# A spline feed-forward stage: pairs of knots side by side in the two 64-row halves, and TensorE takes part of the sum

## The reference, cut to what matters

```python
s = layernorm(x) @ Win + bin_                    # (2048, 64)
for h in range(16):                              # INNER = 16 knots
    g += relu(s * W1[:, h] + b1[:, h]) * W2[:, h]    # elementwise on 2048 x 64
out = (g + b2) @ Wout + bout                     # (2048, 128)
x = x + out
```

## Time and profile before

| what | value |
|---|---|
| timed runs | 2342.31, 2346.17, 2368.61 us (median 2346.17) |
| profiled execution, its own time | 2356.42 us |
| its span in the trace | 2354.6 us |
| TensorE matmuls busy over the span | 1947.0 us, 83% |
| VectorE busy | 1680.3 us, 71% |
| ScalarE busy | 1372.5 us, 58% |
| GpSimd busy | 497.5 us, 21% |
| the two spline stages | 43.44 us and 43.35 us |

### The profile page before, as it was taken

The page is one execution under the profiler, slowest core; times in us unless marked ns, Lnnn a source line. Parts: engine busy times, 40 slices in busy tenths (PEclk is TensorE's granted clock), DMA queues, the critical chain, the costliest instruction groups (busy, mean ns, idle before and its releaser), DMA issues. The chain is left out here.

```text
span 2354.6 us, 39284 instructions
## 1 busy us (share of the span) xinstructions
PE 1947.0 (83%) x13014; PEld 1053.1 (45%) x13014; DVE 1680.3 (71%) x4272; ACT 1372.5 (58%) x2027; POOL 497.5 (21%) x963
## 2 busy tenths in 40 slices
PE   4899899984899984697899899976647999999849
PEld 3433343332567763464333333356424333333348
DVE  6788788737566767567798798642697887988443
ACT  4247767766278875335367677842444467667722
POOL 4101121110266650120100111123101010210233
PEclk9579999985899996797699999978856899999959
DMA  7242130003201000005142020005114402200024
GB/s 226 78 72 27 13 39 1 2 2 125 87 26 40 38 25 1 1 1 164 16 73 38 3 38 2 2 10 198 45 36 144 69 10 34 36 4 1 2 93 176
DMA packets 48058, 117.49 MB, mean 50 GB/s; under 512 B 12400, under 2 KB 21874, under 8 KB 43592
## 3 DMA queue, kind: packets, MB, share of 16 engines
q1 hardware_dynamic: 40260, 100.02, 18.0%
q0 software_dynamic: 5088, 11.24, 1.5%
q10 hardware_dynamic: 2540, 4.09, 0.5%
HBM read 65.96 MB, written 36.20 MB: 43 GB/s over the span
## 5 line engine op out<-in xcount | busy, mean ns | idle before, releaser
L1128 ACT ACTIVATE probs<-score 128x1024 f32<-128x1024 f32 x960 | 823.6, 898 | 431.2 <-PE score L1227 425.8
L1298 DVE TENSOR_REDUCE max_part<-stat 128x1 f32<-128x512 f32 x1152 | 725.0, 684 | 95.0 <-PE stat L1179 87.0
L1241 PE MATMUL pv<-probs,v_ones 128*9 128x512 f32 (+3 forms) x3840 | 460.8, 553 | 0.2 <-ACT out_turned L1121 0.2
L1295 DVE CUSTOM_DVE_ANT_0 masked_scores<-stat,mask_row 128x128 f32<-128x128 f32 (+3 forms) x768 | 347.2, 488 | 144.9 <-PE stat L1179 141.4
L1179 PE MATMUL stat<-first_group_k,first_group_q 64*128 64x512 f32 (+2 forms) x960 | 364.3, 494 | 36.3 <-DVE max_part L1298 12.6
L1179 PE MATMUL stat<-group_k,group_q 64*128 64x512 f32 (+2 forms) x960 | 337.4, 407 | 16.1 <-DVE max_part L1298 7.6
L1179 PEld LDWEIGHTS stat<-first_group_k,first_group_q 64*128 64x128 f32 x960 | 176.3, 215 | 284.2 <-DVE max_part L1298 176.5
L1179 PEld LDWEIGHTS stat<-group_k,group_q 64*128 64x128 f32 x960 | 157.6, 185 | 278.6 <-DVE max_part L1298 162.9
L1227 PE MATMUL score<-first_group_q,first_group_k 64*128 64x512 f32 x960 | 249.6, 420 | 32.0 <-ACT probs L1128 19.5
L1227 PE MATMUL score<-group_q,group_k 64*128 64x512 f32 x960 | 232.2, 423 | 40.1 <-ACT probs L1128 30.8
L1086 POOL TENSOR_SCALAR_AFFINE_SELECT probs<-probs 128x256 f32<-128x256 f32 x384 | 150.2, 408 | 238.3 <-ACT probs L1128 237.1
(11 more groups left out here) (424 smaller groups left out, 2567.8 us busy)
## 6 DMA issues: line engine op xcount, KB each, us to landing
tile_wv<-expert_wv SPq DMA_DIRECT2D x38, 512.0 KB
q_parts<-early_parts_t SPq DMA_DIRECT2D x14, 512.0 KB, 3.7
group_k<-k_parts SPq DMA_DIRECT2D x24, 256.0 KB, 11.8
group_q<-q_parts SPq DMA_DIRECT2D x24, 256.0 KB, 18.4
sorted_rows<-in_c_unused_rows SPq DMA_DIRECT2D x1, 4754.5 KB, 25.2
k_parts<-early_parts_t SPq DMA_DIRECT2D x8, 512.0 KB, 4.6
head_q<-q_parts SPq DMA_DIRECT2D x32, 128.0 KB
head_k<-k_parts SPq DMA_DIRECT2D x32, 128.0 KB
```

What stands on the lines that cost most here:

```text
L1128: nc.scalar.activation(probs[:, n % PSLOTS, :, 0:width], sc[m % 2][:, :, 0:width], ACT.Exp, scale=scale).then_inc(slot_read.sem, 1)
L1241: last = nc.tensor.matmul(acc[32 * h:32 * h + D + 1, f:BANK], v9[:, kt, g * HG + h, :], probs[:, (2 * t + h // 2) % PSLOTS, h % 2, 0:BANK ...
L1295: nc.vector.tensor_tensor_reduce(masked[:, at % 2, 0:width], ring[n % RBANKS][:, 0:width], w["mask_row"][:, BANK - width:BANK], 1.0, NEG, ...
L1298: nc.vector.reduce_max(into, ring[n % RBANKS][:], AX.X).then_inc(stat_used.sem, 1)
```

## The change

The two 64-row halves no longer hold different tokens but different knots of the same tokens. `Win` is loaded twice, side by side (128 columns), so that one matmul for each quarter writes s into both halves of a bank of `spline_in_ps`. Rows 0 to 63 of W1, b1 and W2 hold knots 0 to 7, rows 64 to 127 knots 8 to 15; one 128x512 instruction works on a pair of knots of one quarter. There are 8 pairs times four quarters, again 32 units. They are divided:

- pair 7 (`OWN`) is bent by VectorE itself, straight from PSUM, as max(W1 s, low) with low = -(W1 bin + b1); the constant that this leaves out goes into b2. TensorE sums it.
- pairs 5 and 6 (`BY_PE`) are bent by ScalarE and summed by TensorE: the knot tile is multiplied by `folded` = W2 times Wout, three 128x128 tables which VectorE makes in the stage (with `bias`, `low` and `b2`).
- pairs 0 to 4 (`BY_SUM`) are bent by ScalarE and added by VectorE into one running sum, which waits for its direct predecessor. There is no even and odd sum and no join.

ScalarE reads `spline_in_ps` (PSUM) with a bias that holds bin, so `enter` is gone; its knots of a quarter wait for VectorE's own knot of that quarter (`own_knots`). `spline_in_ps` grows from two banks to four. In each quarter TensorE has four products of 512 tokens (own pair, pair 5, pair 6, sum with `Wout`) that accumulate in one bank over all 128 rows. The four quarters end one after another, and the statistics of a quarter follow in the next quarter's adds. The normalisation order is 0, 1, 2, 3 in place of 0, 2, 1, 3, and TensorE transposes the third quarter ahead of the first feed.

In `experts_stage` three semaphores become one; the five GpSimd instructions and their order stay.

```diff
 rest_loads
-        (w["Win"][:], d["L0_ffn_Win"]),
+        (w["Win"][:, 0:M0], d["L0_ffn_Win"]),
+        (w["Win"][:, M0:], d["L0_ffn_Win"]),
+        (w["b2"][0:M0, :], d["L0_ffn_b2"].rearrange("(m o) -> m o", o=1)),
+        (w["b2"][M0:, :], d["c_pad"][0, 0:M0].rearrange("(m o) -> m o", o=1)),
...
 spline_ffn_stage
+    BY_SUM, BY_PE, OWN = (0, 1, 2, 3, 4), (5, 6), (7,)
+    BENDS = [(q, m) for q in range(NQ) for m in (0, 5, 1, 2, 6, 3, 4)]
...
             @block.tensor
+                def feed(q):
+                    norm.wait(pe, q)
+                    nc.tensor.matmul(sp_in[:, q, :], w["Win"][:], xn_t[:, q * BANK:(q + 1) * BANK], start=True, stop=True).then_inc(fed.sem, 1)
+                def take(q, lhs, weight, first, last):
+                    for i in range(QC):
+                        ins = nc.tensor.matmul(out[:, q, i * P:(i + 1) * P], lhs[:, i * P:(i + 1) * P], weight, start=first and i == 0, stop=last and i == QC - 1)
+                    return ins
+                norm.turn(pe, 0)
+                norm.turn(pe, 1)
+                norm.turn(pe, 2)
                 feed(0)
+                norm.turn(pe, 3)
+                for q in range(1, NQ):
+                    feed(q)
+                pe.wait_ge(tables.sem, tables.at(ALL_TABLES))
+                for q in range(NQ):
+                    for n in range(NO):
+                        pe.wait_ge(own_knots.sem, own_knots.at(NO * q + n + 1))
+                        take(q, own[:, q % 2, n, :], folded[:, n, :], n == 0, False).then_inc(used.sem, 1)
+                    for n, m in enumerate(BY_PE):
+                        pe.wait_ge(knots.sem, knots.at(BEND_AT[q, m] + 1))
+                        take(q, slot(q, m), folded[:, NO + n, :], False, False).then_inc(used.sem, 1)
+                    pe.wait_ge(summed.sem, summed.at(NS * (q + 1)))
+                    take(q, g[:, q % 2, :], w["Wout"][:], False, True).then_inc(out_ready.sem, 1)
...
             @block.scalar
+                def bend(n):
+                    q, m = BENDS[n]
+                    act.wait_ge(own_knots.sem, own_knots.at(NO * (q + 1)))
+                    if n >= SLOTS:
...
+                    nc.scalar.activation(slot(q, m), sp_in[:, q, :], ACT.Relu, bias=bias[:, m:m + 1], scale=w["W1"][:, m:m + 1]).then_inc(knots.sem, 1)
                 def begin(n):
+                    if n == 2:
+                        act.wait_ge(tables.sem, tables.at(BIAS))
+                        for m in range(2):
+                            bend(m)
...
             @block.vector
+                def bend(q):
+                    dve.wait_ge(fed.sem, fed.at(q + 1))
...
+                        nc.vector.tensor_scalar(own[:, q % 2, n, :], sp_in[:, q, :], w["W1"][:, m:m + 1], low[:, m:m + 1], ALU.mult, ALU.max).then_inc(own_knots.sem, 1)
+                def add(q, n):
...
+                        dve.wait_ge(summed.sem, summed.at(NS * q + n))
+                        ins = nc.vector.scalar_tensor_tensor(into, slot(q, m), w["W2"][:, m:m + 1], into, ALU.mult, ALU.add)
...
                 norm.dve(dve)
+                nc.vector.scalar_tensor_tensor(bias[:], w["W1"][:], w["bin"][:, 0:1], w["b1"][:], ALU.mult, ALU.add).then_inc(tables.sem, 1)
+                nc.vector.tensor_scalar(low[:], bias[:], -1.0, None, ALU.mult).then_inc(tables.sem, 1)
...
+                bend(0)
+                for n, m in enumerate(OWN + BY_PE):
+                    ins = nc.vector.tensor_scalar(folded[:, n, :], w["Wout"][:], w["W2"][:, m:m + 1], None, ALU.mult)
+                ins.then_inc(tables.sem, 1)
+                for q in range(NQ):
+                    for n in range(NS):
+                        add(q, n)
+                        if n == 0 and q + 1 < NQ:
+                            bend(q + 1)
+                        if n == NS - 3 and q > 0:
+                            complete(q - 1)
+                        if n == NS - 2 and q > 0:
+                            read(q - 1)
+                    if q > 0:
+                        stats.gather(dve, q - 1)
+                complete(NQ - 1)
+                read(NQ - 1)
+                stats.gather(dve, NQ - 1)
```

More of the change, by code:

```diff
@@ L1354, in _ @@
             def _(pe):
[L1355 to L1363, removed]
@@ L1365, in project @@
-                def project(c):
-                    pe.wait_ge(whole.sem, whole.at(c + 1))
-                    for half in range(2):
-                        at = slice(half * M0, half * M0 + M0)
-                        for i in range(QC):
-                            ins = nc.tensor.matmul(out[:, 2 * half + c, i * P:(i + 1) * P], g[at, c, 0, (INNER // 2) % 2, i * P:(i + 1) * P], w["Wout"][at, :],
-                                                   start=True, stop=True)
-                        ins.then_inc(out_ready.sem, 1)
@@ L1442, in complete, with read @@
                     part = x[:, QC * q:QC * q + QC, :]
                     nc.vector.tensor_tensor(part, out[:, q, :].rearrange("p (i c) -> p i c", c=C), part, ALU.add).then_inc(out_used.sem, 1)
-                    stats.follow(dve, n, out_used)
+                def read(q):
+                    dve.wait_ge(out_used.sem, out_used.at(q + 1))
+                    stats.take(q)
                 norm.dve(dve)
-                for h in range(INNER):
-                    add(0, h)
-                for h in range(2):
-                    add(1, h)
@@ L1451, in _ @@
-                join(0)
-                for h in range(2, INNER):
-                    add(1, h)
-                    if h == 9:
-                        dve.wait_ge(biased.sem, biased.at(1))
-                        complete(0)
-                    if h == 11:
-                        complete(1)
-                join(1)
-                complete(2)
-                complete(3)
-        fed.done(2)
-        s_ready.done(2)
-        whole.done(2)
-        knots.done(2 * INNER)
-        summed.done(2 * INNER)
+                nc.vector.scalar_tensor_tensor(bias[:], w["W1"][:], w["bin"][:, 0:1], w["b1"][:], ALU.mult, ALU.add).then_inc(tables.sem, 1)
@@ new lines, in _ @@
+                dve.wait_ge(tables.sem, tables.at(BIAS))
+                nc.vector.tensor_scalar(low[:], bias[:], -1.0, None, ALU.mult).then_inc(tables.sem, 1)
+                for n, m in enumerate(OWN):
+                    if n > 0:
+                        dve.wait_ge(tables.sem, tables.at(2 + n))
+                    nc.vector.scalar_tensor_tensor(b2[:], bias[:, m:m + 1], w["W2"][:, m:m + 1], b2[:] if n else w["b2"][:], ALU.mult, ALU.add).then_inc(tables.sem, 1)
+                dve.wait_ge(tables.sem, tables.at(OWN_TABLES))
@@ L1468, in spline_ffn_stage @@
+                complete(NQ - 1)
+                read(NQ - 1)
+                stats.gather(dve, NQ - 1)
+        fed.done(NQ)
+        knots.done(len(BENDS))
+        own_knots.done(NO * NQ)
+        summed.done(NS * NQ)
+        tables.done(ALL_TABLES)
+        used.done(NX * NQ)
         out_ready.done(NQ)
```

128 lines of the change are left out of this document (56 added, 72 removed).

## The result

The changed kernel takes **2331.53 us** (median of 14 runs, 2321.97 to 2341.77); the kernel before, run beside it, takes 2351.56 us (14 runs, 2340.64 to 2368.61). The ratio is 0.9922, with a 95% interval from 0.9902 to 0.9942. Of 2351.56 us that ratio is 18.3 us less, the difference of the medians 20.0; 19 were forecast. (The forecast time of 2327 us starts from the median of three runs, 2346.17; the median of 14 is 5.4 us higher, so the time to hold against 2331.53 is the saving and not 2327 itself.) The profiled execution took 2338.46 us (span 2336.7) against 2356.42 before, 17.96 less.

A forecast was written before the change was run, and what follows sets the result against it. VectorE's stream, ending last, was taken to set the spline stage's length. Two stages 9.0 us shorter plus 0.5 us twice behind them make 19 us, from the 2346.17 us median to 2327 us; range 2312 to 2345.

The forecast's parts named there:

- up to the first add: Spline stage opening: first feed, own knot, then `folded` tables held by GpSimd's addition; put at 10.2 us.
- quarter 0: VectorE's adds directly behind each other, with the own knot of quarter 1 and no quarter to complete; 4.1 us.
- quarters 1 and 2: VectorE's adds, own knot, and the completion and statistics of the quarter before; 5.5 us each.
- quarter 3: VectorE's adds and the previous quarter's completion and statistics, without an own knot to make; 4.8 us.
- wait for the last product: End of the spline stage: VectorE waits for TensorE, 2.17 us; a quick product would make the stage 9.9 us shorter.
- GpSimd's hold: Opening: GpSimd's `bout` addition holds VectorE's SBUF-sourced tables but not the PSUM-sourced own knot; 1.3 us either way a stage.
- VectorE's small terms: Prices in the quarters: own knot 0.61 us, dependent add 0.78 us including a 0.03 us semaphore step.
- ScalarE: Spline stage: 28 knots from PSUM at 0.58 us start to start, 16.2 us, off the path.
- The rival of TensorE at 1.2 GHz: Spline stages: TensorE becomes the bound, stage only 3.6 us earlier, 7 us in total, 2339 us; chance 15%.
- What lies behind the stages: Next stages start with a warmer TensorE, so their transposes are quicker; 0.5 us each, twice.
- The extra load: Rest loads: one DMA more on GpSimd's queue, covered by 24.49 us of idle; uncovered, about half a microsecond.
- The two rivals of the attention stages: Attention clock shifts: third stage 4.9 us shorter, part of 26.3 us saved, 2320 (19%); or clock worse, 2349 (6%).

The follow-up runs named there:

- experiment 3: Changed kernel with pairs 5 and 6 returned from TensorE to VectorE's sum; spline stages 41.34 and 41.46 us.
- experiment 4: Changed kernel with one pair more summed by TensorE (pair 4), VectorE summing four; spline stages 31.12 and 31.71 us, timed later at 2323.34 us, ratio 0.9891.
- experiment 5: Changed kernel with even and odd running sums again, both projected by TensorE; spline stages 31.94 and 31.85 us.
- Experiment 1: Changed kernel with GpSimd adding `bout` to only one of 16 row tiles; spline stages 33.53 and 33.22 us, program 2319.55 us in one run.
- experiment 6: Changed kernel with ScalarE bending all eight pairs, VectorE none, TensorE summing pairs 5, 6 and 7; spline stages 32.97 and 32.75 us.
- experiment 7: Kernel before with only the experts stages' three semaphores made one; 2349.6 us against 2346.84, ratio 1.0004.
- experiment 2: Changed kernel with the own pair's product issued four times at quarter weight, 56 matmuls a quarter instead of 32; spline stages 38.74 and 37.89 us.

## Why the prediction was right, step by step

The forecast was 2327 us and 19 us less; the ratio gives 18.3. The stage was to last 34.4 us (43.4 - 9.0) and lasts 34.55 and 34.17. Its parts, from the start of the first stage to the next:

| part | forecast | measured | difference |
|---|---|---|---|
| up to the first add | 10.2 | 9.83 | -0.35 |
| quarter 0 | 4.1 | 4.40 | +0.3 |
| quarters 1 and 2 | 5.5 each | 5.67, 5.66 | +0.35 for both |
| quarter 3 | 4.8 | 4.92 | +0.1 |
| wait for the last product | 2.17 | 1.39 | -0.8 |
| complete, statistics, aggregates | 2.0 | 2.01 | 0 |
| to the next stage | 0.3 | 0.67 | +0.35 |

(The measured wait runs from the last add's end to `complete`; TensorE's row has 1.06 us of it.) The mechanism was right: VectorE's stream sets the stage (experiments 3 to 5). The size is right partly by luck: the quarters were 0.8 us too cheap and the way to the next stage 0.35, the last wait 0.8 too dear and the opening 0.35. These errors can be named.

**GpSimd's hold.** Forecast: `bout` from 4.9 to 9.4 us into the stage, the own knot free, the tables held to 9.4. Measured: 4.89 to 9.43, the own knot 0.81 us, the tables done at 9.9 where 10.2 was forecast. The own knot began at 6.4 us instead of 6.8, since the first feed took 1.37 us where 1.91 had been taken. Reading the 0.42 and 2.01 us of the earlier trace rows as a difference between a PSUM and an SBUF source was right. Experiment 1 prices the hold at 1.0 us a stage, where 1.3 had been the bound.

**VectorE's small terms** were too low. The own knot costs 0.73 us start to start (545.38 to 546.11), not the 0.61 of other PSUM instructions. The dependent add costs 0.86 (quarter 0: four in 3.31, less one length of 0.74, by 3), not 0.78; experiment 5 shows 0.66 for the same add without the dependency. The 0.03 us for the step was read from the earlier trace rows, where no start comes behind its predecessor's end: the statistics at 576.27 begin before `complete` ends (575.66 + 0.69 = 576.35), so these rows could not show it. Together this makes the +0.8 us of the quarters.

**The last wait.** It was taken as 2.17 us because the clock of the stage had been 0.54. In the kernel after, it was 0.87 over the stage and the last eight products took 1.06; the 9.9 us with a quick last product, named there as the other value, was the right one for this term, less what the quarters cost more.

**ScalarE** was put at 0.58 us a knot from the one difference 549.71 to 550.29 in the earlier trace rows, which was between an `enter` with a bias and a knot. A knot from PSUM costs 0.67 ((17.52 - 0.77) / 25 in the row of 26). It stays hidden, 4.7 of 5.67 us, but it is nearer to the bound than was said, and experiments 4 and 6 run into it.

**The rival of TensorE at 1.2 GHz** fell as a sum: 39 us a stage was its mark, and VectorE never waits for `spline_out_ps` before the end. The granted clock is 0.99 in the middle of the stage, with TensorE 11.34 of 16.00 us busy and idle for 1.3 to 1.8 us in each of the first three quarters. Yet the mechanism is not absent. In both stages of the kernel after, and in its second execution, the products behind the third quarter's sum ran at the low level. It costs next to nothing here, and VectorE's quarter has 2 us of room for it. Experiment 1, with the same wait of 1.81 us in both its stages, has the dip in the second and not in the first, where the products behind that wait took 1.16 and 1.06. This is its TensorE timeline in the second stage:

```profile
908.98 1.71 PE L1375 MATMUL spline_out_ps<-spline_folded,spline_own_knot 128*128 128x128 f32 x8
```

VectorE's last wait there is 1.10 us with the dip and 1.03 without it. What brings the dip in the one stage and not in the other is open. The Trainium skill (TensorE: Matmul & The Clock Gate, "A second HAM failure mode: psum-queue depth-cycling") warns of such gaps; the traces here agree in that one place in a stage and disagree in the other quarters, and leaving it out of the sum proved right for this kernel.

**What lies behind the stages** was put at 0.5 us each for a warmer TensorE. Up to the second pair of `w_qkv_r` products the retention stage takes 6.77 us after (565.25 to 572.02), 8.14 in the execution of before and 7.42 in that of experiment 7: 0.65 to 1.4 less. Both executions of the changed kernel show it (6.77 twice). The linear stage takes the same up to the second pair of its 128x256 products (8.87 against 8.88), but up to the third pair 9.54 and 9.52 us where the kernel before has 10.13 and experiment 7 9.99, so 0.45 to 0.6 less. At the openings the term of 0.5 us is thus there. The retention stages as wholes, 318.99 and 323.14 with the old spline, 320.52 with the new one, don't show even its sign, so that the 1 us stays in the total is not shown. The extra load was not tried by itself; its cover held, since GpSimd's queue still idles 25.53 and 24.86 us behind the loads, where it was 24.49. The first stretch, in which it lies, took 528.6 to 539.5 us in the executions that have it and 535.06 and 537.22 in those that don't.

**The two rivals of the attention stages** rested on a scatter of 6 us between them, and this was too small. These are that stage in before, after and after again, 2816 matmuls each:

```profile
1067.27:1569.30 502.03, 445.36 (x2816) 194.09 (x2816) 393.31 (x1012) 324.22 (x425) 64.58 (x178) 0.93 0.20 39
```

```profile
1038.80:1549.81 511.01, 455.29 (x2816) 198.58 (x2816) 393.44 (x1011) 323.87 (x425) 64.33 (x178) 0.90 0.19 39
```

```profile
1038.01:1540.32 502.31, 446.60 (x2816) 194.37 (x2816) 393.04 (x1012) 323.97 (x425) 64.64 (x178) 0.92 0.20 39
```

VectorE and ScalarE do the same work to within 0.4 us; TensorE's busy time and clock differ, and so does the length, by 9 us between two executions of one kernel. Over the eleven profiled executions, of nine kernels, the second and third attention stages took from 501.6 to 511.9 us. Both rivals of this kind are thus part of the scatter of any run, not a consequence of the change; no run shows the change to move it.

The 0.35 us at the end of the first stage (0.67 instead of 0.32 in the second) are open: experiments 1 and 2 have them too, experiments 3 to 6 don't, and the second stage has 0.32 in every execution. Of what experiments 3 to 6 show for the first stage, 0.35 is thus this item; their second stages are the better comparison.

## What to carry to other kernels

When a vector engine adds scaled tiles that are then multiplied by a matrix, fold the scale into the matrix and let the matmuls accumulate: here 0.112 us a matmul, eight for a tile, hidden, take the place of a dependent add of 0.86 us, until the engine that makes the tiles is level with the adder (with five of eight on VectorE there was still room, with four the engines were nearly level). Ask of each unit which engine has room for it: the pair that VectorE made for itself here was cheaper on ScalarE. Count a move between engines by the stream that is last, and price each instruction by its start-to-start distance in the very form that it will have: the source, the scale and bias, and above all whether it waits for its predecessor. To judge a change of 1% in a long program, compare the changed stages in two traces, and ask of every other stage how much it differs between two executions of the same kernel.

## What the runs showed of the hardware that was not expected

- An add of 128x512 costs 0.66 us start to start when it is independent and 0.86 when it waits for the add just before it, though the instruction itself lasts 0.745: 0.11 us pass from its end to the start of the one that waits for it, not 0.03.
- ScalarE's knot costs 0.67 us a piece from PSUM and 0.71 from SBUF (28 in 19.89): the change of source gives 0.04, not the 0.13 that was read from one pair of rows.
- An instruction of VectorE with its source in PSUM isn't slowed by a running GpSimd addition (0.81 us with and without it); the one with its source in SBUF ends only behind it (2.59 us instead of 0.54 in experiment 6, ending 0.28 us after GpSimd's).
- TensorE, 11.34 of 16.00 us busy in bursts with up to 1.8 us between them, had a granted clock of 0.99 over these 16 us, but ran at the low level for some 3 us behind the third wait of each stage.
- The attention stages, untouched and with the same instructions, differ by up to 10 us each from execution to execution, with the granted clock between 0.90 and 0.93.
